# Inner blocks of banded attention scores as two column tiles of 64, 192 columns each

## What is computed

```python
scores = jnp.einsum('bqhd,bkhd->bhqk', q, k) / jnp.sqrt(d)          # 8 heads of 16
band = jnp.abs(idx[:, None] - idx[None, :]) <= local_size            # local_size = 64
scores = jnp.where(band[None, None], scores, neg)
attn = jax.nn.softmax(scores, axis=-1)
o = jnp.einsum('bhqk,bkhd->bqhd', attn, v).reshape(n, t, e)
o = relu(o @ w_out.T + b_out) * encodings                            # then mixed by w_ct
...
x = x + attention(layernorm(x))
x = x + experts(layernorm(x))                                        # top 2 of 16, and a shared one
```

## Time and profile before

| | |
|---|---|
| median of 3 runs | 720.66 us (717.82 to 722.0) |
| profiled execution, its own time | 721.22 us |
| its span | 719.0 us |
| mean granted TensorE clock | 0.966 of full |
| PE busy | 660.6 us (92%) |
| DVE busy | 390.9 us (54%) |
| ACT busy | 367.1 us (51%) |
| POOL busy | 427.8 us (60%) |

### The profile page before, as it was taken

The page is one execution under the profiler, slowest core; times in us unless marked ns, Lnnn a source line. Parts: engine busy times, 40 slices in busy tenths (PEclk is TensorE's granted clock), DMA queues, the critical chain, the costliest instruction groups (busy, mean ns, idle before and its releaser), DMA issues.

```text
span 719.0 us, 14013 instructions
## 1 busy us (share of the span) xinstructions
PE 660.6 (92%) x4134; PEld 323.6 (45%) x4134; DVE 390.9 (54%) x1424; ACT 367.1 (51%) x689; POOL 427.8 (60%) x653
## 2 busy tenths in 40 slices
PE   3679899999999999988999999899999989999992
PEld 1345455555555555544445545333333333333330
DVE  3789888888888888851124786322222222222220
ACT  4248667777777767656323222344444344444441
POOL 5248788888888887766110001137767567758763
PEclk8579999999999999999899999999999999999997
DMA  6544544554554433212495943434665566544530
GB/s 211 158 120 114 143 123 130 152 138 133 137 137 137 114 108 102 76 31 79 146 405 189 421 156 120 146 81 99 108 139 128 122 134 123 113 105 83 88 50 0
DMA packets 65275, 95.25 MB, mean 132 GB/s; under 512 B 18345, under 2 KB 43049, under 8 KB 63145
## 3 DMA queue, kind: packets, MB, share of 16 engines
q1 hardware_dynamic: 50544, 66.49, 30.2%
q0 software_dynamic: 9600, 18.89, 14.8%
q10 hardware_dynamic: 5058, 8.99, 3.7%
HBM read 50.99 MB, written 19.14 MB: 98 GB/s over the span
## 4 chain that ended last, share of the span: by engine, by line
PE 67%; DVE 13%; issue 7%; POOL 5%; DMA 4%; ACT 1%; SPq 1%; POOLq 0%; ACTq 0%; DVEq 0%
PE bank L774 18%; PE bank L805 8%; DVE bank L1171 7%; PE bank L600 5%; PE bank L761 4%; PE bank L565 4%; PE bank L793 4%; PE bank L651 4%; PE bank L583 3%; PE bank L754 3%; PE bank L739 3%; PE bank L785 2%; PE bank L659 2%; PE bank L620 2%; PE bank L672 2%
## 5 line engine op out<-in xcount | busy, mean ns | idle before, releaser
L1171 DVE CUSTOM_DVE_ANT_0 bank<-bank,cb 128x192 f32<-128x192 f32 (+1 forms) x512 | 186.0, 418 | 32.8 <-PE bank L565 32.5
L942 ACT ACTIVATE wgu<-bank 128x384 f32<-128x384 f32 (+1 forms) x256 | 125.6, 547 | 45.9 <-PE bank L583 45.4
L774 PE MATMUL bank<-wgu,rowsT 128*64 x320 | 145.9, 599 | 0.0
L776 PE MATMUL bank<-X,rowsT 128*64 128x512 f32 x320 | 145.9, 598 | 0.0
L1404 DVE TENSOR_TENSOR act_in<-act_in,bank 128x256 f32<-128x256 f32 x56 | 23.6, 421 | 201.1 <-ACT act_in L1061 175.7
L565 PE MATMUL bank<-wgu 96*128 96x192 bf16 (+1 forms) x512 | 95.0, 271 | 20.2 <-DVE wgu L1171 14.5
L456 POOL TENSOR_SCALAR_AFFINE_SELECT wgu<-wgu 128x512 f32<-128x512 f32 (+1 forms) x128 | 74.5, 582 | 47.2 <-ACT wgu L942 46.9
L499 POOL DMA_INDIRECT rows<-xn_rows,gather_i x40 | 44.4, 1109 | 88.6 <-DVE gate_of L1399 61.8
L517 POOL DMA_INDIRECT out<-y_out,scatter_i x40 | 65.5, 1638 | 30.6 <-issue 23.0
L517 POOL DMA_INDIRECT out<-y_out,scatter x40 | 58.5, 1462 | 42.0 <-DMA out<-y_out,scatter_i 25.6
L565 PEld LDWEIGHTS bank<-wgu 96*128 96x128 bf16 x512 | 45.2, 101 | 79.9 <-DVE wgu L1171 39.3
(11 more groups left out here) (174 smaller groups left out, 1116.0 us busy)
## 6 DMA issues: line engine op xcount, KB each, us to landing
wgu<-wgu SPq DMA_DIRECT2D x190, 128.0 KB, 2.5
wgu<-w_gu SPq DMA_DIRECT2D x16, 1024.0 KB, 13.1
X<-w_d SPq DMA_DIRECT2D x16, 512.0 KB
out<-y_out ACTq DMA_DIRECT2D x17, 256.0 KB, 3.3
X<-x SPq DMA_DIRECT2D x16, 256.0 KB, 3.3
wgu<-ctx SPq DMA_DIRECT2D x16, 256.0 KB, 3.2
xn_rows<-xn SPq DMA_DIRECT2D x16, 256.0 KB, 2.4
rows<-xn_rows ACTq DMA_DIRECT2D x16, 256.0 KB, 3.5
```

Of the source, the lines that this page charges most:

```text
L774: mm(gb[k.buf][0:GROUP, :], rowsT[:, k.buf, c, 0:GROUP], wgu[:, bass.ds(e * 2048 + 512 * c, 512)], start=(c == 0), stop=(c == 3))
L776: last = mm(gb[k.buf][GROUP:P, :], rowsT[:, k.buf, c, GROUP:P], gu_half[:, k.buf, 512 * c:512 * c + 512], start=(c == 0), stop=(c == 3))
L942: nc.scalar.activation(probs[j % 4][:, 2 * half:2 * half + 2, 0:w], s2[half][:].rearrange("p (j c) -> p j c", j=2)[:, :, 0:w], ACT.Exp, sc ...
L1171: last = v.tensor_tensor_reduce(o, o, cb[:, B_MASK + off:B_MASK + off + w], 1.0, MASKED * 2.0, ALU.add, ALU.max, rowmaxes[n % 2][:, h + i, ...
```

## The change

For inner blocks, both scores are computed as two column tiles of 64 output rows with 192 columns each, from the 64 queries (or keys) and the 192 that they can see, instead of one product of 128 rows by 256 columns. Edge blocks stay. For the first scores both tiles write columns 0 to 191 of their half of the partitions, the maximum is taken over 192 columns, and its mask is a new strip `B_NEAR`, which reads the same for both tiles. For the shifted scores the second tile writes 64 columns further, so that what ACT, POOL and `attend_values` read keeps its place and size; the two banks are set to zero once. The strip takes the place of unused constants, and its copy on DVE is split in three.

```diff
+B_NEAR = B_ZERO
 def scores(n, j, half):
...
+                    if w < 2 * P:
+                        last = mm(s1[half][:, 256 * i:256 * i + w], ...)
+                        continue
+                    for a in (0, LOCAL):
+                        last = mm(s1[half][a:a + LOCAL, 256 * i:256 * i + NEAR],
+                                  qstack[n % RING][0:STACK, h, P * blk + a:P * blk + a + LOCAL],
+                                  kstack[n % RING][0:STACK, h, lo + a:lo + a + NEAR], start=True, stop=True)
 def shifted_scores(n, j, half):
...
+                    for a in (0, LOCAL):
+                        o = 256 * i + a
+                        last = mm(s2[half][a:a + LOCAL, o:o + NEAR],
+                                  kstack[n % RING][0:STACK + 3, h, P * blk + a:P * blk + a + LOCAL],
+                                  qstack[n % RING][0:STACK + 3, h, lo + a:lo + a + NEAR], start=True, stop=True)
...
+            for half in range(2):
+                v.memset(s2[half][:], 0.0).then_inc(s2_clear, 1)
 def maximum(n, j, half):
+                band = mask(blk)
+                if w == 2 * P:
+                    w, band = NEAR, cb[:, B_NEAR:B_NEAR + NEAR]
...
-            v.tensor_copy(cb[:], cb_f).then_inc(setup, 1)
+            v.tensor_copy(cb[:, 0:B_NEAR], cb_f[:, 0:B_NEAR]).then_inc(setup, 1)
+            for a in (0, LOCAL):
+                v.tensor_copy(cb[a:a + LOCAL, B_NEAR:B_NEAR + NEAR],
+                              cb_f[a:a + LOCAL, B_MASK + a:B_MASK + a + NEAR]).then_inc(near_ready, 1)
```

More of the change, by code:

```diff
@@ L36 @@
 LOCAL = 64
+NEAR = 3 * LOCAL
 QB = T // P
@@ L256, in xattn_moe_kernel @@
         v_ready = sem("v_ready")
+        s2_clear = sem("s2_clear")
+        near_ready = sem("near_ready")
         s1_ready, rowmax = sem("s1_ready"), sem("rowmax")
@@ L564, in scores @@
                     h = 4 * hg + 2 * half + i
-                    last = mm(s1[half][:, 256 * i:256 * i + w],
-                              qstack[n % RING][0:STACK, h, P * blk:P * blk + P],
-                              kstack[n % RING][0:STACK, h, lo:lo + w], start=True, stop=True)
+                    if w < 2 * P:
+                        last = mm(s1[half][:, 256 * i:256 * i + w],
+                                  qstack[n % RING][0:STACK, h, P * blk:P * blk + P],
+                                  kstack[n % RING][0:STACK, h, lo:lo + w], start=True, stop=True)
+                        continue
[3 more added lines that the diff above has]
+                                  kstack[n % RING][0:STACK, h, lo + a:lo + a + NEAR], start=True, stop=True)
                 last.then_inc(s1_ready, 1)
@@ L576, in shifted_scores @@
                         pe.wait_ge(ones_set, 1)
+                        pe.wait_ge(s2_clear, 2)
                     if n == 1:
@@ L582, in shifted_scores @@
                     h = 4 * hg + 2 * half + i
-                    last = mm(s2[half][:, 256 * i:256 * i + w],
-                              kstack[n % RING][0:STACK + 3, h, P * blk:P * blk + P],
-                              qstack[n % RING][0:STACK + 3, h, lo:lo + w], start=True, stop=True)
+                    if w < 2 * P:
+                        last = mm(s2[half][:, 256 * i:256 * i + w],
+                                  kstack[n % RING][0:STACK + 3, h, P * blk:P * blk + P],
+                                  qstack[n % RING][0:STACK + 3, h, lo:lo + w], start=True, stop=True)
+                        continue
+                    for a in (0, LOCAL):
[3 more added lines that the diff above has]
+                                  qstack[n % RING][0:STACK + 3, h, lo + a:lo + a + NEAR], start=True, stop=True)
                 last.then_inc(s2_ready, 1)
@@ L1165, in maximum @@
                 h = 4 * hg + 2 * half
+                band = mask(blk)
+                if w == 2 * P:
+                    w, band = NEAR, cb[:, B_NEAR:B_NEAR + NEAR]
                 if j == 0 and half == 0:
                     after(dve, m_step, 4 * (n - 2) + 2)
+                    if n == 0:
+                        dve.wait_ge(near_ready, 2)
                 dve.wait_ge(s1_ready, 2 * UNITS * n + 2 * j + half + 1)
@@ L1170, in maximum @@
                     o = s1[half][:, 256 * i:256 * i + w]
-                    last = v.tensor_tensor_reduce(o, o, cb[:, B_MASK + off:B_MASK + off + w], 1.0, MASKED * 2.0,
+                    last = v.tensor_tensor_reduce(o, o, band, 1.0, MASKED * 2.0,
                                                   ALU.add, ALU.max, rowmaxes[n % 2][:, h + i, blk:blk + 1])
```

## The result

The changed kernel takes 730.22 us (median of 4 runs, 724.86 to 731.89) where the kernel before takes 721.24 beside it; the ratio is 1.0122, with an interval of 1.0076 to 1.0169. So the change costs between 5 and 9 us. The forecast was 727.0, in a range of 719 to 736.

A forecast was written before the change was run, and what follows sets the result against it. DVE's maxima were taken to bound each period's first half, PE the second; 0.5 us of seams for 12 sequences (+6.0) and +0.5 at the start made +6.5, 721.22 to 727.7, 727 as a median, range 719 to 736.

The forecast's parts named there:

- What bounds the kernel: Steady attention: 19.10 us a sequence, some 7.4 us bounded by DVE's maxima, then 11.7 us where PE waits for nobody.
- ACT and POOL keep their sizes: ACT and POOL, whole kernel: their work stays the same size, so no term was given for them.
- "faster" rival: Steady stage: bf16 tiles of 64 beside 128 drain nothing, about -0.8 us for each of 12 sequences, 711 us; chance 0.12.
- The drain at a seam: PE, where the array's division changes between groups: 0.09 us lost at each seam.
- The first load: PE, first weights after a seam into tiles: 0.05 us bare, with bounds of 0.01 and 0.05.
- The period's sum: Steady stage: between 0.4 and 0.56 us more a sequence, taken as 0.5 for 12 sequences, +6.0 us.
- low bounds: PE's seams with a bare first load of 0.01 us: +0.40 us a sequence in the second half, +0.88 in the first.
- 1.10 of room: First half of a period: PE's waits sum to 1.10 us a sequence, set against the seams' +1.20 (low bound +0.88).
- 19.5 to 19.7: Steady stage, sign that the forecast is right: the channel mix recurs every 19.5 to 19.7 us.
- rival with cheaper seams: Steady stage: narrow load hides, or 64 to 32 is no seam; 0.1 to 0.3 us a sequence, 723 us; chance 0.25.
- rival of loads that don't hide: PE's tile pairs: loads don't hide, pairs take 0.11 us, +1.4 us more a sequence, 744 us; chance 0.08.
- The start: Start of the kernel: two more memsets and a copy split in three on DVE cost +0.5 us.

The follow-up runs named there:

- one192: Changed kernel with one product of 128 rows by 192 columns replacing the two tiles in both scores, omitting 64 columns; 722.79 us, 1.0060 of the kernel before.
- q_dve: Kernel before with the third part of q moved from POOL to DVE, one unit later; 718.23 us, 0.9976 of the kernel before.
- one_q: The kernel with single 128 by 192 products (64 columns left out), third part of q moved to DVE; 712.56 us, 0.9895, total no measure; period 18.13.
- s_q_dve: Against the kernel before: tiles in the first scores only, and the third part of q moved from POOL to DVE; 718.33 us, 0.9982.
- x_only: Changed kernel with tiles in the shifted scores only, first scores and maxima back at 256 columns; 724.97 us, 1.0072 of the kernel before.
- s_only: Changed kernel with tiles in the first scores and their maxima only, shifted scores back at 128 by 256; 720.59 us, 1.0012 of the kernel before.
- early: Changed kernel with tiles in the first two sequences only; 722.34 us, 1.0053 of the kernel before.
- warm: Changed kernel plus 20 unused bf16 products of 128 by 512 on PE in units 0 to 9; 720.63 us, 1.0001 of the kernel before.
- again: The changed kernel itself, measured in twelve more runs; 725.02 us, 1.0073 of the kernel before.
- late: Changed kernel with tiles only from the third sequence on; 723.65 us, 1.0069 of the kernel before.

## Why the prediction was right, and where it was not

**What bounds the kernel: half right.** The two halves of a period are there, and DVE's first half was on the chain. But the chain shows one loop, the one that ended last. POOL's loop of 19.10 lay level with it, and the prediction put it down as "ACT and POOL keep their sizes", without asking what POOL allows. Nor does PE wait for nobody in the second half: there the 0.08 of POOL's loop are hidden within four products of L583. So its "faster" rival, 711 us with seams that cost nothing, could not be: one192 has no seams and stays at 19.10. Shown by one192, q_dve and one_q together.

**The drain at a seam: right.** 0.09 us predicted at three kinds of seam from f32 tiles; measured 0.09 from 128-wide bf16 to tiles of 64, and 0.10 out again.

**The first load: the mis-sized term.** "I take 0.05, since a bf16 load is not quicker for being narrower" failed; it measured 0.024, near the low bound. The Trainium skill (TensorEngine Tiling (Array Packing), Restrictions) says that column tiling switches Fast Weight Load off, and with the load rule of TensorE: Matmul & The Clock Gate 53 ns would be bare, an estimate. The trace does not bear the estimate out: 24 ns show. The loads of L601 themselves last 106 to 110 ns in this stretch, so most of each is hidden. The durations in the earlier trace rows were those of loads that lie beside products, and say little of what is bare.

**The period's sum: right by its low bounds.** They gave 0.40 in the second half and 0.88 against 1.10 of room in the first: 0.18 a sequence. Measured 0.19, with PE at 40.00 of 40. The prediction took 0.5, because it put the first half at 0 instead of at what its own low bound gave, and the second at the upper price. Over twelve sequences that makes 2.3 us where "+6.0" stood. Its check on the period, "19.5 to 19.7", was missed at 19.29, which was the mark of its rival with cheaper seams. Pairs of tiles run side by side and follow each other at 0.08, as said, so the rival of loads that don't hide is out.

That the low bounds come out so close is in part luck, for two things that they leave out nearly cancel. PE alone, if it waited for nobody, would have taken 19.10 less 1.10 and less the 0.08 above before: 17.92. Tiles in the scores add 0.88 by the low bound and 0.11 for eight first loads of 0.024 in place of 0.01: 18.91, where s_q_dve measured 18.94. A unit of shifted scores, from the first L570 to the second, went from 0.61 to 0.71 (167.63 to 168.34), which is 0.40 for four: 19.31 in all, against 19.29.

**The parts apart.** x_only costs 0.27, less than the 0.40 of the second half by its low bound; the loop of PE and DVE before was at most 19.02 (q_dve), so 0.08 of the 0.40 went unseen beneath POOL's 19.10; the last 0.05 is not explained. s_only should have won 0.22 by that sum; it is held at 19.12 by POOL's loop. With the loop relieved, s_q_dve stops at 18.94, which by the account above is PE alone with its seams. That is only 0.08 under the loop of PE and DVE in q_dve.

**The start: not told.** "+0.5" measured 0.0, within some 1.6 us either way, so it is neither borne out nor refuted.

**The fill: missed.** Nothing was priced between the start and full stride. There the changed kernel's clock rose at 59 to 62 us in both its profiled executions, and at 45 before. That a late rise costs is shown twice. Against early the same instructions took 3.3 us longer by the clock alone. And warm, with an earlier clock, has 1.0001 where again had 1.0073, some 5 us, and no overlap of the intervals; the raw medians, of two chips, differ by 4.4. Why the clock rises late is open. That tiles leave PE emptier there is not what the rows say: from 30 to 46 us PE was busy for 12.01 of 16 in again and for 10.90 before. And early, s_only and the changed kernel ran the same instructions on PE up to 51 us, and had their rise at 51, 51 and 62. In late and x_only, and in q_dve, which has no tiles, it came at 48 to 51. So something other than the order of PE's instructions has a large part in the rise, though both profiled executions of the changed kernel had it late. Of the 7.4 us in the profiled fill, 2.7 are in early as well (91.3 against 88.6) and 3.3 are the later rise; how the 2.7, and the loss of a typical execution, divide between the tiles and other causes stays open.

So the total of 725 to 730 fell where 727.0 was predicted, but as 2 us of seams and 3 to 7 of fill, not as 6 of seams and 0.5 of start. The direction follows from the seams; that the number fits is luck.

## What to carry to other kernels

Ask of each engine that isn't on the chain how long its own loop takes: a second loop of nearly the same length hides the gain of every edit to the first, and only an edit of both shows it. Price column tiles with both seams of every run: here they cost 0.2 us a run, where the narrower streams of eight products gave 0.1. Where a change touches a fill, look at the granted clock there, in more than one execution: here a few products that nobody needs were cheaper than a rise at 59 to 62 us, and gained next to nothing in the fill of a kernel that had its rise at 46.

## What the runs showed of the hardware

- A seam from tiles of 64 to tiles of 32 costs what one to 128 wide does. In PE's timeline of the changed kernel:

```profile
177.78 0.36 PE L575 MATMUL bank<-wgu 96*64 96x192 bf16 x4
178.06 0.50 PE L595 MATMUL bank<-wgu 99*128 99x192 bf16 x4
178.50 0.36 PE L575 MATMUL bank<-wgu 96*64 96x192 bf16 x4
178.78 1.07 PE L618 MATMUL bank<-wgu 128*32 128x256 f32 x16
```

Both runs of four L575 take 0.28 to the next start, the one ahead of 128-wide L595, the other ahead of 32-wide L618. That is 0.17 of columns and some 0.11 of seam. From 177.78 to 178.78 the columns (0.34 and 0.34) and three seams of 0.10 make 0.98 of the 1.00 measured.
- At a seam into tiles, the load of 64 columns in bf16 was bare for 0.024 us.
- The time of the clock's rise in the fill moved between 45 and 62 us from kernel to kernel, and 20 products that nobody needs brought it to 28 to 29 us. In the changed kernel this was worth some 5 us of 725 by the ratios, 4.4 by the medians.
- The same PE instructions, up to 51 us, were followed by a rise at 51.5 us in early and by one some 10 us later in the changed kernel.
